# A two-layer graph network on one core: the self term of the nodes moved out of the node loop

## The chip, the cores and the metric

One NeuronCore of a Trainium2 chip runs the whole program. Its engines are TensorE (PE; matmuls, with the weight loads as PEld beside them), VectorE (DVE), ScalarE (ACT), GpSimd (POOL) and the queue engine SyncE (SP); they run on their own and meet at semaphores. The metric is the device time of one execution in microseconds (us), and lower is better. The three runs of the kernel before took 2241.53, 2242.63 and 2242.85 us; the median is 2242.63.

## The reference

Two graph layers over 100000 nodes of 64 features and 50000 edges. The edges come sorted by destination. Every layer starts with a layer norm and a maximum with zero.

```python
h = jnp.maximum(_layernorm(x, axis=-1), 0.0)
# layer 0
msg = h[src] * edge_weight[:, None]
agg = segment_sum(msg, dst, num_segments=100000)
x = x + (agg @ W_neigh + b_neigh) + h @ W_self.T      # h @ W_self.T is the self term
# layer 1: pools edge_attr by src; u[batch] is u[0] for all nodes
seg_sum, seg_max, cnt = segment_sum / segment_max / count of edge_attr over src
seg_mean = seg_sum / max(cnt, 1);  seg_max = where(cnt > 0, seg_max, 0)
z = relu(concat([seg_sum, seg_max, seg_mean, u0]) @ W1 + b1)
out = x + z @ W2 + b2
```

The second layer reads `edge_attr` and not the node features, so the output of a node is `x` + its self term + the weighted messages of its incoming edges + the pooled term of its outgoing edges.

## The kernel before, in words

Edges are taken in tiles of 128 and groups (`g`) of 8 tiles, 49 groups (`MG`). Nodes are taken in windows of 128 and groups of 8 windows, 98 groups (`WG`). The program has a first block (rank, sort and messages) and a second block (the node loop), and a third for rare overflows that has hardly any work here.

**First block.** GpSimd gathers the rows `x[src]` of the first 8 edge groups (`gather`, `EARLY = RX = 8`), then scatters all 391 tiles of edge attributes into `by_win`, ordered by window of the source node (`scatter`, L598), then gathers the other groups (L592). A scatter of group g needs its target rows, which the *rank* works out: `rank_dve`, `rank_pe` and `rank_act` run a loop over 50 groups, in which one-hot matmuls count the digits of the window numbers (histogram, h), transpose the one-hots (t), compare codes (eq, same), and a scan on VectorE and a look-up matmul turn counts into positions. After the rank, VectorE makes the first 8 message groups; once all scatters have landed it sorts the windows in 7 batches (`sort_batch`: 12 rounds of max-of-8 and the flags that drive the segment scans), and then makes the other 41 message groups as their rows come in. `message_of(g)` is: centre (L397 to L399), square on ScalarE (L417), sum (L404), root on ScalarE (L421), reciprocal times edge weight, scale and maximum (L409 to L412), four transposes on TensorE (L427), evacuation on ScalarE (L442), matmul with `W_neigh` (L806), and a split of the result into three bf16 parts (`keep`, L433 to L436), stored to `message`. A tally of destination windows (`one_hots(..., "dst")`, L797) runs in the same function and gives the table of starts at the end.

**Second block, the node loop.** A step g handles 1024 nodes. SyncE loads `x` and 8 chunks of messages; GpSimd loads the pooled edge rows, slots and flags; ring of 4. On VectorE the step is: `scans` (L997 to L1000: segment sums, maxima, means), `permute(g+1)` (L988), `norm_scale(g+1)` (L409, L412), `picks` (L1016, L1018: one-hots of destinations), `centre(g+2)`, `finish(g-1)` (L1031: adds PSUM to x), `select` (L1006: one-hots that put pooled rows in place), `value` (L1039), `norm_sum(g+2)`, `value_left` (L1045), `value_low` (L1050). On TensorE: `hidden` (L1110, the matmul with W1), `edges(g-1)` (L1141), `permute(g+1)` (L1100), `turn(g+1)` (L1151, transposes of h), `outer` (L1122, the matmul with W2), `selves(g+1)` (L1160, the self term), `neighbours` (L1131). On ScalarE: relu of the hidden layer, evacuation of the transposes, square, high part (L1209), root, middle part (L1213), and the store of the step before. Engines take their instructions in program order. What the second block reads and writes of PSUM and of the x ring is guarded by semaphores, so that an instruction in the queue holds up all behind it.

## Time and profile before

| | |
|---|---|
| profiled execution | 2241.82 us, span of its instructions 2240.1 us |
| busy, share of the span | PE 56%, PEld 48%, DVE 72%, ACT 22%, POOL 49% |
| instructions on DVE | 3568 |
| mean granted TensorE clock | 0.641 of full speed |
| HBM | read 138.46 MB, written 62.73 MB |

The busy shares are means over stages that differ. In the 40 equal slices of the page, TensorE shows nothing in slices 9 to 12 and VectorE nothing in 10 and 11, and VectorE is at eight tenths through the second half. GpSimd is at seven tenths through the first 19 slices and at two after them. How to read it: first the stages (windows of time) with the busy time of every engine in each, then inside a stage the timeline, for who starts when the other ends.

### The profile page before, as it was taken

The numbers are of one execution on the slowest core, as the hardware profiler recorded it, in microseconds if no ns is written. First come the engines' busy times: TensorE is split into PE (matmuls) and PEld (weight loads), VectorE is DVE, ScalarE is ACT, GpSimd is POOL, SyncE is SP. The second block draws the span as 40 slices with busy tenths as digits, with TensorE's granted clock in tenths as the row PEclk, the third lists the DMA queues.
The fourth block names the chain that finished last, engine by engine and source line by source line (L and its number), as shares of the span: only waits on it lengthen the run. The fifth ranks groups of instructions, "written<-read, shape, count | busy, mean of one in ns | idle before, by whom it ended". The sixth has DMA issues, their size and how long they took to land. (4 is left out here: it accounts for less than half of the span.)

```text
span 2240.1 us, 41882 instructions
## 1 busy us (share of the span) xinstructions
PE 1258.9 (56%) x14884; PEld 1073.5 (48%) x14885; DVE 1617.5 (72%) x3568; ACT 494.4 (22%) x888; POOL 1101.9 (49%) x1404
## 2 busy tenths in 40 slices
PE   4566565400001444433277777777777777777775
PEld 3444443300000333322266666667676666666665
DVE  5766767810068888766488888888888888888886
ACT  1221211100000211111132333333332333333332
POOL 7777777777773777777222222222222222232220
PEclk7565555555555555555577777777777777777776
DMA  9700000100063222222545555555555555555551
GB/s 263 95 13 13 12 13 13 55 28 13 13 154 82 76 76 79 73 61 67 104 109 122 125 119 120 125 123 121 124 119 123 123 118 124 118 123 126 119 123 32
DMA packets 405256, 203.62 MB, mean 91 GB/s; under 512 B 370375, under 2 KB 377799, under 8 KB 404407
## 3 DMA queue, kind: packets, MB, share of 16 engines
q1 hardware_dynamic: 254792, 93.02, 19.4%
q0 software_dynamic: 46976, 72.79, 14.3%
q10 hardware_dynamic: 103312, 35.54, 6.3%
q8 instruction: 101, 1.65, 0.3%
q14 instruction: 75, 0.61, 0.1%
HBM read 138.46 MB, written 62.73 MB: 90 GB/s over the span
## 5 line engine op out<-in xcount | busy, mean ns | idle before, releaser
L592 POOL DMA_INDIRECT xg_all<-in_x_dram,idx_src x391 | 385.9, 987 | 149.4 <-issue 118.3
L598 POOL DMA_INDIRECT by_win<-rows,idx_win x391 | 391.2, 1000 | 127.3 <-issue 127.3
L969 POOL DMA_DIRECT2D rows<-by_win x98 | 52.2, 532 | 782.4 <-DVE arena L1000 753.7
L1110 PE MATMUL ps<-arena,w1r 32*128 32x192 f32 x2352 | 214.2, 526 | 267.8 <-DVE arena L1000 264.6
L1110 PEld LDWEIGHTS ps<-arena,w1r 32*128 32x128 f32 x2352 | 164.6, 302 | 280.1 <-DVE arena L1000 276.6
L974 POOL DMA_DIRECT2D rows<-flag_d x392 | 214.4, 554 | 13.7 <-issue 13.6
L1122 PE MATMUL ps<-w_sb,arena 128*96 128x64 f32 x1568 | 185.8, 285 | 0.0
L1122 PEld LDWEIGHTS ps<-w_sb,arena 128*96 128x96 f32 x1568 | 184.4, 203 | 0.0
L1197 ACT ACTIVATE arena<-ps,hbias 128x768 f32<-128x768 f32 x98 | 88.3, 901 | 413.0 <-PE ps L1110 413.0
L417 ACT ACTIVATE sq<-xc 128x512 f32<-128x512 f32 x147 | 91.6, 623 | 364.7 <-DVE xc L399 364.7
L427 PE MATMUL ps<-ident,h 128*128 128x128 f32 x196 | 54.6, 434 | 174.4 <-DVE h L412 174.4
L1141 PEld LDWEIGHTS ps<-arena 96*128 96x128 bf16 x2352 | 126.4, 129 | 45.4 <-issue 45.4
L1141 PE MATMUL ps<-arena 96*128 96x64 bf16 x2352 | 140.5, 239 | 3.0 <-DVE arena L1050 3.0
L1160 PE MATMUL ps<-wsT,hT 128*128 128x128 f32 x784 | 138.9, 333 | 0.7 <-ACT hT L1202 0.7
L815 PE MATMUL ps<-ident,arena 96*112 96x96 f32 x14 | 5.0, 462 | 216.0 <-DMA arena<-by_win 216.0
L1039 DVE TENSOR_TENSOR arena<-ps,c0b 96x512 f32<-96x512 f32 x98 | 67.3, 686 | 78.6 <-PE ps L1122 71.2
L1160 PEld LDWEIGHTS ps<-wsT,hT 128*128 128x128 f32 x784 | 123.5, 239 | 1.1 <-ACT hT L1202 1.1
L714 DVE SCALAR_TENSOR_TENSOR left<-ps,iota_n 112x96 f32<-112x96 f32 x7 | 1.8, 258 | 167.7 <-PE ps L815 166.8
L1018 DVE TENSOR_TENSOR arena<-iota_n,arena 96x1024 bf16<-96x1024 f32 x98 | 119.6, 1221 | 3.4
L427 PEld LDWEIGHTS ps<-ident,h 128*128 128x128 f32 x196 | 35.0, 217 | 179.7 <-DVE h L412 179.7
L806 PE MATMUL ps<-wn,hT 128*128 128x128 f32 x392 | 101.6, 441 | 33.6 <-ACT hT L442 33.6
L1006 DVE TENSOR_TENSOR arena<-iota_n,end_n 96x1024 bf16<-96x1024 f32 x98 | 119.1, 1215 | 0.0
(191 smaller groups left out, 2840.9 us busy)
## 6 DMA issues: line engine op xcount, KB each, us to landing
rows<-message SPq DMA_DIRECT2D x784, 36.4 KB, 2.0
rows<-flag_d POOLq DMA_DIRECT2D x392, 72.0 KB, 2.6
rows<-in_x_dram SPq DMA_DIRECT2D x97, 256.0 KB, 3.1
out_dram<-rows ACTq DMA_DIRECT2D x97, 256.0 KB, 2.8
message<-m_row SPq DMA_DIRECT2D x48, 388.0 KB, 2.3
zeros<-slot_d POOLq DMA_DIRECT2D x98, 144.0 KB, 2.9
by_win<-zeros ACTq DMA_DIRECT2D x12, 808.5 KB, 10.6
arena<-by_win SPq DMA_DIRECT2D x7, 1386.0 KB, 9.4
```

What stands on the lines that cost most here:

```text
L417: nc.scalar.activation(sq[:, :, :], xc[b][:, :, :], ACT.Square).then_inc(ln["squared"], 1)
L427: last = nc.tensor.transpose(ps[bank][:, P * k:P * k + P], h[b][:, 2 * k:2 * k + 2, :].rearrange("p a c -> p (a c)"), ident[:, :])
L592: nc.gpsimd.indirect_dma_start(out=xg[g % RX][:, t % GT, :], out_offset=None, in_=x, in_offset=bass.IndirectOffsetOnAxis(ap=idx_src[:, t:t ...
L598: nc.gpsimd.indirect_dma_start(out=by_win, out_offset=bass.IndirectOffsetOnAxis(ap=idx_win[0:parts, t:t + 1], axis=0), in_=rows[0:parts, t ...
L806: last = nc.tensor.matmul(ps[1 + b][:, P * k:P * k + P], hT[b][:, k, :], wn2[:, :], start=True, stop=True)
L974: pool.dma_start(f_in[b][DE * q:DE * q + DE, :, :], two.unsqueeze(0).to_broadcast([DE, 3, 2 * SL])).then_inc(a_loaded[b], 16)
L1006: nc.vector.tensor_tensor(sel[g % 2][:, :, :], iota_n[0:SL, :].unsqueeze(1).to_broadcast([SL, GT, P]), end_n[:, g * GT:g * GT + GT].unsque ...
L1018: nc.vector.tensor_tensor(pick[c][0:CH, :, :], iota_n[0:CH, :].unsqueeze(1).to_broadcast([CH, GT, P]), near[c][:, :].unsqueeze(2).to_broad ...
L1110: last = nc.tensor.matmul(ps[z_bank[q]][:, 0:2 * SL], w1r[DE * q:DE * q + DE, j, :], part[DE * q:DE * q + DE, :], start=(j == 0), stop=(j ...
L1122: last = nc.tensor.matmul(ps[v_bank][0:SL, D * k:D * k + D], hid[:, SL * k:SL * k + SL], w2_sb[:, :], start=True, stop=True)
L1141: last = nc.tensor.matmul(ps[o_bank[c]][:, D * k:D * k + D], sel[c][:, k, :], v_part[:, k, n, :], start=False, stop=(k == GT - 1 and n == ...
L1160: nc.tensor.matmul(ps[o_bank[g % 2]][:, P * k:P * k + P], hT[g % 2][:, k, :], wsT2[:, :], start=(k == 0), stop=False)
```

## The change

The self term no longer stands in the node loop. A list of steps of two kinds is made (`steps_of`): "node" steps, 98 of them, which norm a group of 1024 nodes, multiply with `W_self` and store `x` + self term to a new table `s0_d`; and "edge" steps, the 49 message groups. Both run through the same functions (`centre`, `spread_of`, `scale_of`, `keep`; `turn` and `project` on TensorE; `square`, `relu`, `turned`, `root` on ScalarE). 61 node steps stand beside the rank, one or two per group from group 8 on; 37 stand between the edge steps behind it. A result is kept three steps after it was begun (`LAG = 3`). For node steps the scaling and the maximum are eight ScalarE instructions, one per tile of 128x64.

The rank is rewritten as well (`place_dve`, `place_pe`, `place_act`): straight code over 49 groups, the histogram is copied to four blocks of partitions, so that transposes and look-up need two wide matmuls instead of eight and sixteen narrow ones, and the tally of destinations runs in it. The sorts stand between edge steps (groups 9, 14, ... 39), the sort's row buffer is single and its other half holds node rows. The table of starts is worked out right after the rank. The node loop loads `s0_d` instead of `x` and has neither norm nor transposes nor self matmul; its `select` stands behind `value`.

The core of the diff (places with the same pattern left out):

```diff
+        s0_d = dram("s0_d", [WG * GT * P, D])
...
+            for g in range(MG):
+                chain(g)
+                same_of(g)
+                if g >= 1:
+                    place(g - 1)
+                if g + 2 < MG:
+                    spread(g + 2)
+                beside(g)
+                tallied(g)
...
+            count(0)
+            operands(0)
+            for g in range(MG):
+                if g + 1 < MG:
+                    count(g + 1)
+                second(g)
+                if g + 1 < MG:
+                    operands(g + 1)
+                beside(g)
+                if g >= 1:
+                    tally(g - 1)
...
+        def place_act(act, r, beside):
+            for g in range(MG):
+                if g >= 1:
+                    beside(g - 1)
+                b = g % 2
+                act.wait_ge(r["h"], g + 1)
...
+                for q in range(4):
+                    last = nc.scalar.activation(hist_all[b][DIGIT * q:DIGIT * q + DIGIT, :, 1:GT + 1],
+                                                h_ps.rearrange("p k l -> p l k"), ACT.Copy)
+                last.then_inc(r["w"], 1)
...
+        LAG = 3
+        NODES_AHEAD = 3
...
+            for g in range(FIRST_BESIDE, MG):
+                for _ in range(1 + g % 2):
+                    beside[g].append(todo.popleft())
...
+                def step(n):
+                    if n >= 1:
+                        scale_of(n - 1)
+                    centre(n)
+                    if n >= LAG:
+                        keep(n - LAG)
+                    spread_of(n)
...
+                for kind, g in tail_steps:
+                    step(step_of[kind, g])
+                    if kind == "edge" and g in SORT_AT:
+                        sort_batch(SORT_AT.index(g))
...
+                def relu(n):
+                    kind, g = steps[n]
+                    if kind == "edge":
+                        return
...
+                    for k in range(GT):
+                        last = nc.scalar.activation(h[b][:, k, :], xc[b][:, k, :], ACT.Relu, scale=stat[b][:, 2, k:k + 1])
+                    last.then_inc(ln["h"], 1)
...
+                def step(n):
+                    if n >= 1:
+                        relu(n - 1)
+                    square(n)
+                    if n >= 1:
+                        turned(n - 1)
+                    root(n)
...
-                        sp.dma_start(x_in[b][:, :, :], nodes_of(x, g)).then_inc(x_loaded[b], 16)
+                    sp.dma_start(x_in[b][:, :, :], nodes_of(s0_d, g)).then_inc(x_loaded[b], 16)
...
                 for g in range(WG):
                     scans(g)
                     if g + 1 < WG:
                         permute(g + 1)
-                        norm_scale(dve, own, (g + 1) % 2, cn0 + g + 2, None).then_inc(w["h"], 1)
                     picks(g)
-                    if g + 2 < WG:
-                        centre(g + 2)
                     if g >= 1:
                         finish(g - 1)
+                    value(g)
                     select(g)
-                    value(g)
-                    if g + 2 < WG:
-                        norm_sum(dve, g % 2, cn0 + g + 3)
                     value_left(g)
                     value_low(g)
...
-                        turn(g + 1)
                     outer(g)
-                    if g + 1 < WG:
-                        selves(g + 1)
                     neighbours(g)
```

How the change moves instructions, at three places. First ScalarE in the rank. Before, a group of the rank on ScalarE (`hist` and `ohT` are the copies of the histogram and of the transposed one-hots):

```order
L368 ACTIVATE hist<-ps 32x32x8
L63 ISA
L373 ACTIVATE ohT<-ps 32x512
L374 ACTIVATE ohT<-ps 32x512
L63 REGISTER_ALU
```

After, a group with two node steps and the head of the next (`h`, `sq`, `hT`, `stat`: scaled rows, squares, transposed rows, statistics of the norm):

```order
L432 ACTIVATE hist<-ps 32x32x8 x4
L438 ACTIVATE ohT<-ps 128x256
L1124 ACTIVATE h<-xc,stat 128x64 x8
L1106 ACTIVATE sq<-xc 128x512
L1132 ACTIVATE hT<-ps 128x512
L1111 ACTIVATE stat<-stat,eps_t 128x8
L1124 ACTIVATE h<-xc,stat 128x64 x8
L1106 ACTIVATE sq<-xc 128x512
L1132 ACTIVATE hT<-ps 128x512
L1111 ACTIVATE stat<-stat,eps_t 128x8
L432 ACTIVATE hist<-ps 32x32x8 x4
```

Two whole norm steps now stand between one group's histogram copies and the next one's.

Second, TensorE in the rank. Before, one group (`later` and `identh` give the comparison operands, `oh` the one-hots, `same` the comparisons, `begin_p` the table that is looked up):

```order
L326 MATMUL ps<-later,identh 128x512
L329 MATMUL ps<-identh,code_s 128x128 x4
L326 MATMUL ps<-later,identh 128x512
L329 MATMUL ps<-identh,code_s 128x128 x4
L336 MATMUL ps<-oh_lo,oh_hi 32x32 x8
L341 MATMUL ps<-identb,oh_hi 32x128 x8
L346 MATMUL ps<-ones_b,same 128x1 x8
L351 MATMUL ps<-begin_p,ohT 128x32 x16
```

After, a group with two node steps (L1042 is the self matmul, L1029 the transposes of h, L405 the tally):

```order
L379 MATMUL ps<-oh_lo,oh_hi 32x32 x8
L384 MATMUL ps<-identb,oh_hi 128x128 x2
L394 MATMUL ps<-ones_b,same 128x1 x8
L398 MATMUL ps<-begin_p,ohT 128x128 x2
L366 MATMUL ps<-later,identh 128x512
L370 MATMUL ps<-identh,code_h_win 128x128 x4
L366 MATMUL ps<-later,identh 128x512
L370 MATMUL ps<-identh,code_h_win 128x128 x4
L1042 MATMUL ps<-wsT,hT 128x128 x4
L1029 MATMUL ps<-ident,h 128x128 x4
L1042 MATMUL ps<-wsT,hT 128x128 x4
L1029 MATMUL ps<-ident,h 128x128 x4
```

The transposes of a node step stand behind the group's comparison operands and behind the self matmul of the node step before.

Third, VectorE in the node loop. Before, the part of a step between `permute` and the left part:

```order
L409 RECIPROCAL stat<-stat 128x8
L412 SCALAR_TENSOR_TENSOR h<-xc,stat 128x512
L1016 TENSOR_TENSOR arena<-rows,first_of 96x8
L1018 TENSOR_TENSOR arena<-iota_n,arena 96x1024
L397 TENSOR_REDUCE stat<-rows 128x8
L398 TENSOR_SCALAR stat<-stat 128x8
L399 TENSOR_TENSOR xc<-rows,stat 128x512
L1031 TENSOR_TENSOR rows<-rows,ps 128x512
L1006 TENSOR_TENSOR arena<-iota_n,end_n 96x1024
L1039 TENSOR_TENSOR arena<-ps,c0b 96x512
L404 TENSOR_REDUCE stat<-sq 128x8
L1045 TENSOR_TENSOR arena<-arena 96x512
```

After, the same part:

```order
L1292 TENSOR_TENSOR arena<-rows,first_of 96x8
L1294 TENSOR_TENSOR arena<-iota_n,arena 96x1024
L1304 TENSOR_TENSOR rows<-rows,ps 128x512
L1312 TENSOR_TENSOR arena<-ps,c0b 96x512
L1282 TENSOR_TENSOR arena<-iota_n,end_n 96x1024
L1318 TENSOR_TENSOR arena<-arena 96x512
```

The six instructions of the norm are gone, and the comparison against `end_n` (`select`) has moved from ahead of `value` (now L1312) to behind it.

## Rows read from the trace of the kernel before

**Rows 1.** Windows of the first half: us, busy (count) by engine, PEclk, DMA, GB/s

```profile
0.00:1083.00 1083.00, 409.82 (x3516) 310.35 (x3517) 664.82 (x1886) 147.17 (x300) 785.15 (x816) 0.53 0.27 63
480.00:560.00 80.00, 0.00 (x0) 0.00 (x0) 0.00 (x0) 0.00 (x0) 58.68 (x62) 0.50 0.06 13
```

**Rows 2.** Windows of the node loop; busy: PE, PEld, DVE, ACT, POOL

```profile
1113.74:2216.49 1102.75, 837.81 (x11228) 753.59 (x11228) 931.58 (x1644) 342.66 (x580) 303.77 (x564) 0.75 0.53 119
...
1612.77:1623.48 10.71, 7.69 (x116) 6.92 (x116) 9.64 (x19) 3.54 (x6) 3.23 (x6) 0.84 0.60 132
1623.48:1636.23 12.75, 10.61 (x116) 9.61 (x116) 9.62 (x19) 3.54 (x6) 3.23 (x6) 0.60 0.54 116
```

**Rows 3.** Timeline, a message step: start us, duration us, engine, line, operation

```profile
740.89 0.20 DVE L409 RECIPROCAL stat<-stat 128x8 f32<-128x8 f32 x1
...
741.93 0.68 DVE L397 TENSOR_REDUCE stat<-xg_all 128x8 f32<-128x512 f32 x1
742.07 1.11 PE L427 MATMUL ps<-ident,h 128*128 128x128 f32 x4 [3.48 <-DVE h L412]
...
743.22 0.60 ACT L442 ACTIVATE hT<-ps 128x512 f32<-128x512 f32 x1 [5.42 <-PE ps L427]
...
743.46 0.46 DVE L269 TENSOR_TENSOR oh_hi<-iota_d,hi_b_dst 128x256 bf16<-128x256 bf16 x1
...
743.87 2.07 PE L806 MATMUL ps<-wn,hT 128*128 128x128 f32 x8 [0.69 <-ACT hT L442]
...
745.09 0.30 ACT L421 ACTIVATE stat<-stat,eps_t 128x8 f32<-128x8 f32 x1 [0.75 <-DVE stat L404]
...
745.98 0.18 DVE L706 COPY m_row<-dst_f 128x8 f32<-128x8 f32 x1 [0.93 <-PE ps L806]
...
748.58 0.20 DVE L409 RECIPROCAL stat<-stat 128x8 f32<-128x8 f32 x1
```

**Rows 4.** Timeline of a short step of the node loop

```profile
1618.07 0.66 PE L1151 MATMUL ps<-ident,h 128*128 128x128 f32 x4
...
1618.57 1.49 PE L1122 MATMUL ps<-w_sb,arena 128*96 128x64 f32 x16
...
1620.10 0.69 DVE L1039 TENSOR_TENSOR arena<-ps,c0b 96x512 f32<-96x512 f32 x1
...
1621.48 0.69 DVE L1045 TENSOR_TENSOR arena<-arena 96x512 f32<-96x512 f32 x1
```

**Rows 5.** Timeline from the last split to the first scan, VectorE

```profile
1079.59 0.69 DVE L436 TENSOR_TENSOR m_row<-rest,m_row 128x512 bf16<-128x512 f32 x1
...
1100.81 0.67 DVE L397 TENSOR_REDUCE stat<-rows 128x8 f32<-128x512 f32 x1
...
1107.93 0.19 DVE L1054 CAST arena<-biasb 128x64 bf16<-128x64 f32 x1
...
1113.74 0.55 DVE L997 TENSOR_TENSOR_SCAN arena<-rows,ps 128x192 f32<-128x192 f32 x1
```

**Rows 6.** Timeline of one group of the rank

```profile
207.45 0.61 PE L326 MATMUL ps<-later,identh 128*128 128x512 f16 x1
...
207.56 0.42 DVE L302 TENSOR_TENSOR prod<-ps,oh_lo 128x256 f32<-128x256 f32 x1 [1.31 <-PE ps L351]
...
209.26 0.17 DVE L312 SCALAR_TENSOR_TENSOR idx_win<-pos_g,trash 128x8 f32 x1
...
209.27 0.40 PE L336 MATMUL ps<-oh_lo,oh_hi 128*32 128x32 bf16 x8
...
209.87 0.37 ACT L368 ACTIVATE hist<-ps 32x256 f32<-32x256 f32 x1 [5.22 <-PE ps L336]
210.22 1.29 DVE L287 TENSOR_TENSOR same<-ps,code_h_win 128x512 bf16<-128x512 f32 x2 [0.79 <-DVE idx_win L312]
...
211.63 0.75 DVE L293 TENSOR_TENSOR_SCAN begin<-chain_mask,hist 32x288 f32<-32x288 f32 x1
```

**Rows 7.** Window from the first sort to the end of the seventh

```profile
626.56:722.16 95.60, 9.11 (x26) 5.64 (x26) 78.22 (x351) 0.00 (x0) 52.00 (x55) 0.50 0.52 115
```

More of the change, by code:

```diff
@@ L1 @@
 import math
+from collections import deque
 from contextlib import ExitStack
@@ new lines, in beside @@
+                def beside(g):
+                    for st in beside_rank[g]:
+                        step(step_of[st])
+                place_dve(dve, own, r_win, hg, beside)
+                dve.sem_inc(made["counts"], 1)
+                dve.wait_ge(loaded["next"], 16 * 2)
+                own(nc.vector.tensor_scalar(next_i[:, :], next_i[:, :], 7, None, ALU.arith_shift_right))
+                own(nc.vector.tensor_tensor(near_f[:, :], next_i[:, :], code_i[:, 0:NT], ALU.is_lt))
+                own(nc.vector.tensor_reduce(falls[:, :], near_f[:, :], AX, ALU.add))
@@ new lines, in project @@
+                def project(n):
+                    kind, g = steps[n]
+                    bank, weights = (o_node, wsT2) if kind == "node" else (m_of[g % 2], wn2)
+                    pe.wait_ge(ln["hT"], n + 1)
+                    if kind == "node" and g >= 1:
+                        pe.wait_ge(ln["kept"], step_of["node", g - 1] + 1)
+                    if kind == "edge" and g >= 2:
+                        pe.wait_ge(ln["kept"], step_of["edge", g - 2] + 1)
+                    for k in range(4):
+                        last = nc.tensor.matmul(bank[:, P * k:P * k + P], hT[n % 2][:, k, :], weights[:, :],
@@ L860, in _, with beside @@
+                def beside(g):
+                    for st in beside_rank[g]:
+                        step(step_of[st])
+                place_act(act, r_win, beside)
+                for st in tail_steps:
+                    step(step_of[st])
+                relu(len(steps) - 1)
+                turned(len(steps) - 1)
                 act.wait_ge(made["starts"], 4)
```

600 lines of the change are left out of this document (364 added, 236 removed).

## The prediction

> **What bounds the kernel now.** I read the busy time by stages first. Up to 1083 us, in the stages that rank the edges, sort the windows and make the messages, VectorE is busy 664.8 us, so 418 us of it stand empty [rows 1]. In that half GpSimd is never out of work for long: with every other engine idle it issues 62 indirect transfers in 80 us, 1.29 us each [rows 1], and 2 x 391 of them make about 1010 us. GpSimd's queue therefore sets the end of the first half, and VectorE has room beside it, if the room can be used. From the first scan of the node loop (1113.74) to the last (2216.49) there are 97 steps in 1102.75 us, 11.37 each [rows 2]. Here no engine is full: VectorE 931.6, TensorE 837.8. The timeline of a step shows a ring: scans, hidden matmuls, second matmul, value, left part, low part, scans again. It comes in two lengths, 10.71 at a mean granted clock of 0.84 and 12.75 at 0.60 [rows 2], two short and one long in turn: (2 x 10.7 + 12.75) / 3 = 11.38. TensorE is granted 2.4 GHz or 1.2 GHz; it falls to the low level in the three us in which it waits for VectorE, and in the long step it does not come back before the second matmul.
>
> **The change in the node loop.** Gone per step are, on VectorE, two reductions and a subtract of 0.67 to 0.69, the scaling of 0.69, and two small operations, some 3 us; on TensorE the transposes (0.66 at the high clock, 1.11 at the low [rows 3, 4]) and the self matmul; on ScalarE square, root and evacuation. What is it worth on the ring? VectorE's removed work stands before `value`, where VectorE now waits for the outer matmul anyway: nothing. The self matmul comes behind the outer one and TensorE idles after it: nothing. The transposes stand between permute and outer. The outer matmul starts 1618.57, transposes 1618.07 [rows 4]; without them it can start about 0.4 earlier (0.7 in a long step, where they take 1.11). But the order is turned too: `select`, a comparison of 96x1024, stood before `value` and now stands between `value` and the left part. Before, the left part started 1.38 behind value (1620.10 to 1621.48 [rows 4]), because ScalarE's high part was waited for. With `select` between, that is 0.61 (the issue distance) + 1.14 = 1.75, 0.37 later. So the short step stays 10.7, and the long one becomes 12.75 - 0.7 + 0.37 = 12.4. The mix of short and long steps depends on how the steps fall against the clock; I keep one long in three to four: 11.2 on average, **-16 us** for 97. Bounds: all short 97 x 0.67 = -65, all long 97 x (12.4 - 11.37) = +100.
>
> Before the loop, the norms of nodes 0 and 1 (from 1100.81 to 1107.93 [rows 5]) fall away, **-7**. The last part of a message is stored at 1080.3, the first scan starts 33.5 later [rows 5]; that becomes 26.4, perhaps 3 less, since the table of starts is no longer written last.
>
> **The first half: what a node step costs beside the rank.** 98 node steps move there: 61 into groups 8 to 48 of the rank (one in the even, two in the odd, so 21 and 20), 37 between the messages. A node step is 3.1 us of VectorE: reciprocal 0.2, centring 1.53 (741.93 to 743.46 [rows 3]), the reduction of squares 0.68, the add 0.68. By busy time it would fit: 98 x 3.1 = 304 in 418. But each step is a chain over three engines with little between. VectorE reciprocal 0.2; ScalarE scales eight tiles of 128x64. No row has that form: the nearest are 128x8 at 0.30 [rows 3] and 128x512 evacuated at 0.60 [rows 3], so one takes 0.30 to 0.60, by the slope between them 0.34, and eight overlap by 0.1 each: 2.0 (bounds 1.6 and 4.8; nearest to the small one). Then transposes 1.1, evacuation 0.60, root 0.30 [rows 3], and only then the next step's reciprocal: 4.4 with handoffs.
>
> In the rank ScalarE's program has the node step *before* the histogram copies of the next group, and VectorE's next group begins by waiting for them. The ring of a group with one node step, from the end of one `place` to the next: TensorE's counts and look-up 0.7 (they wait for `place`, since the look-up's PSUM has one buffer), comparison operands 1.8 (207.45 to 209.27 [rows 6]), projection 2.07 and transposes 1.11 [rows 3] = 5.7; ScalarE evacuation 0.6, root 0.3, four histogram copies of 0.37 [rows 6] less overlap 1.3; with handoffs 8.0. Then VectorE: copy 0.2, scan 0.75, multiply 0.42, comparison 1.29, `place` 207.56 to 209.43 = 1.87 [rows 6], less overlap 4.4. Sum **12.4**. A second node step adds another chain of 4.4: **16.8**. Groups 8 to 48: 21 x 12.4 + 20 x 16.8 = 596, less 14 for stretches in which TensorE gets the high clock: 582. Groups 0 to 7 have no node step and cost VectorE's own 6.2; they start later than before, at about 30, because the weights must land first (an estimate, 20 to 40); so group 8 starts at 80 and the rank ends at **662**. GpSimd's scatters, which would be through at 97 + 391 x 1.32 = 613, wait for indices from about group 30 on and end some 10 behind the rank. GpSimd stops being the bound.
>
> **Messages, nodes and sorts.** The falls, the tallies and the starts go first: 12. Then, on VectorE, a step behind an edge step costs 1.04 scale + 1.53 + 2.60 split (745.98 to 748.58) + 0.68 + 0.34 waiting for the root (it starts as the reduction ends [rows 3]) = 6.2: before, the split stood between reduction and reciprocal and hid the root. A step behind a node step costs the chain of 4.4. 37 pairs x 10.6 + 12 x 6.2 = 467. Seven sorts, 95.6 us in a row before [rows 7], hide a root wait each: 93. Together 560, so the last message is at 1222 + 12 = 1234; its own tail (scale, transposes, evacuation, projection, split) 8: **1242**. GpSimd's gathers, 327 x 1.28 = 419 from 672, end at about 1100 and are paced by VectorE's ring of eight. The node rows (256 KB in and out a step) move on queues that are mostly empty here; nothing.
>
> Sum: first scan 1242 + 26.4 = 1268, against 1113.7: +154. With the loop's -16: +138. The span 2240.1 becomes 2378; the profiled execution has 1.7 around its span, so **2380 us**. The median of the three runs, 2242.63, stands 0.8 above the profiled 2241.82, which matters to nothing here.
>
> **Rivals.** *A, the room is used.* If the engines overlap across steps better than I read (ScalarE's copies early, relu short), VectorE's busy time is the measure: rank 49 x 6.0 + 61 x 3.1 = 483, done before the scatters end at 613; then edges 8 to 48, 31 nodes and the sorts, 41 x 5.85 + 31 x 3.1 + 93 = 429 behind the first late gather at 623: 1052, first scan 1086, 28 earlier. With the loop 2240 - 28 - 16: **2198**. For it: 418 us of empty VectorE, and the steps are written three deep. Against: every handoff above is a wait on the step just before. *B, TensorE is granted the high clock through the rank.* Its 5.7 us of a group shrink by 2.3, 41 times, and the transposes by 0.4, 37 times: 2380 - 109 = **2270**, still slower. Before, the mean in the rank was hardly above the low level. *C, the node loop loses the clock.* TensorE has nearly 2 us less work in a step of nearly the same length. In the rows a step in which the high level is missed before the outer matmul is the 12.75 one; if all were missed, 97 x 12.4 replaces 97 x 11.2: **2496**. The decision falls where the hidden matmuls and the edges behind them no longer win the high level. The Trainium skill, TensorE: Matmul & The Clock Gate, "What's actually happening", says that the low clock is the default and activity releases it; by that, taking the transposes and self matmuls out speaks for C. The trace agrees so far that the fall comes after idling; whether the matmuls left suffice no row shows. *D, the change does nothing on balance*: A's first half lost in part, within 0.2%.
>
> **How the numbers follow.** Forecast 0.55, its own range 2300 to 2440 (relu at 1.6 or 2.6 us: 98 times, -40 or +60; the loop's mix -49 to +60 around). A 0.24, B 0.10, C 0.08, D 0.03. About 0.2% is what a measurement here can tell from no change. Faster 0.24, same 0.03, slower 0.73. The range must reach into A: 2190 leaves some 0.11 of it outside, 2450 leaves C: 0.19 in all.
>
> **What would show it.** In the profile after: histogram copies on ScalarE that start right behind a root, in groups some 12 and 17 us apart; GpSimd idle during the scatters waiting for VectorE's index, with the last scatter near 670; first scan near 1268; eight scalings of 128x64 in about 2.0; loop steps of 10.7 and 12.4, with VectorE waiting for the outer matmul longer than before. The forecast is wrong if the groups with two node steps take 11 us or less, or if the scatters still end near 613; it is wrong in the loop if the short step is under 10.3 or no two lengths are left.

## The result, and the profile of the changed kernel

The changed kernel takes 2423.31 us (median of 4 runs, 2419.35 to 2424.96), the kernel before 2242.74 (4 runs beside it, 2241.53 to 2244.96). The ratio is 1.0801, 95% interval 1.0783 to 1.082: slower by 181 us where 137 were forecast. The page of the profiled execution begins so:

```profile
span 2420.6 us, 39452 instructions
...
PE 1291.7 (53%) x13560; PEld 1085.0 (45%) x13561; DVE 1604.2 (66%) x3454; ACT 697.3 (29%) x1766; POOL 1095.5 (45%) x1407
```

VectorE, the busiest engine, does 1604 us of work in a span of 2421. That is 13 us less than before (1617.5), and no engine is full. The loss therefore is not VectorE's work but waiting, and the stages say where. The windows (us, busy and count of PE, PEld, DVE, ACT and POOL, PEclk, DMA share, GB/s) of the first half up to the first scan of the node loop, of the rank, of the stretch of messages, nodes and sorts, and of the loop:

```profile
0.00:1308.16 1308.16, 599.33 (x3384) 477.36 (x3385) 936.46 (x2371) 485.53 (x1472) 792.61 (x843) 0.56 0.41 94
...
80.00:726.00 646.00, 304.23 (x2054) 240.78 (x2055) 411.72 (x1035) 272.11 (x865) 386.31 (x392) 0.55 0.28 61
...
740.00:1285.00 545.00, 265.15 (x1061) 215.30 (x1061) 459.61 (x1152) 193.23 (x554) 322.02 (x328) 0.53 0.43 110
...
1308.16:2396.90 1088.74, 685.70 (x10064) 601.62 (x10064) 657.20 (x1067) 209.56 (x291) 302.94 (x564) 0.71 0.53 121
```

The first scan comes at 1308.16 instead of 1113.74 [rows 1, 5]: 194 us later. The loop takes 1088.74 for its 97 steps instead of 1102.75 [rows 2]: 14 us less, 11.22 a step, with 274 us less work on VectorE. In the rank, GpSimd is busy for 386 of 646 us, and its group of scatters now names VectorE's index as what it waits for (busy, mean ns | idle before, most of it for):

```profile
L792 POOL DMA_INDIRECT by_win<-rows,idx_win x391 | 386.6, 989 | 259.7 <-DVE idx_win L340 137.4
...
L1124 ACT ACTIVATE h<-xc,stat 128x64 f32<-128x64 f32 x784 | 197.8, 334 | 221.2 <-DVE stat L896 221.2
```

The distances between the starts of `place` are 5.7 to 5.9 for groups without a node step, 12.7 for one with one, and 18.1 to 20.4, mostly 19, for one with two (the first ones after group 7 are shorter, 10.1 and 15.3). The timeline of a group with two, which runs from 478.90 to 498.03, from its second reciprocal (L896) on (start, duration, engine, line, operation, [idle before, released by]):

```profile
487.46 0.20 DVE L896 RECIPROCAL stat<-stat 128x8 f32<-128x8 f32 x1 [2.69 <-ACT stat L1111]
487.70 2.02 ACT L1124 ACTIVATE h<-xc,stat 128x64 f32<-128x64 f32 x8 [0.27 <-DVE stat L896]
...
489.34 0.68 DVE L910 TENSOR_TENSOR arena<-arena,ps 128x512 f32<-128x512 f32 x1
...
490.17 2.00 PE L1042 MATMUL ps<-wsT,hT 128*128 128x128 f32 x8 [3.56 <-DVE arena L910]
...
491.96 1.06 PE L1029 MATMUL ps<-ident,h 128*128 128x128 f32 x4
...
493.06 0.60 ACT L1132 ACTIVATE hT<-ps 128x512 f32<-128x512 f32 x1 [2.82 <-PE ps L1029]
493.55 0.29 ACT L1111 ACTIVATE stat<-stat,eps_t 128x8 f32<-128x8 f32 x1
493.74 1.51 ACT L432 ACTIVATE hist<-ps 32x256 f32<-32x256 f32 x4
...
495.29 0.20 DVE L320 COPY hist<-begin 128x32 f32<-128x32 f32 x1 [3.66 <-ACT hist L432]
...
498.03 0.41 DVE L334 TENSOR_TENSOR prod<-ps,oh_lo 128x256 f32<-128x256 f32 x1
```

Two things are to be seen. The scalings (L1124) are done at 489.72, but the transposes of the node (L1029) start at 491.96: on TensorE the self matmul (L1042) of an earlier node stands in front of them, and it waits for VectorE's `keep` (L910, ends 490.02), which frees the one PSUM buffer of the result. And VectorE waits 3.66 us for the histogram copies (L432), which on ScalarE stand behind evacuation and root of the last node step. VectorE is busy for 6.45 of these 10.57 us:

```profile
487.46:498.03 10.57, 3.67 (x24) 3.15 (x24) 6.45 (x14) 5.08 (x16) 2.65 (x3) 0.79 0.26 56
```

A short step of the loop, to be laid beside [rows 4]:

```profile
1617.17 1.57 PE L1387 MATMUL ps<-w_sb,arena 128*96 128x64 f32 x16
...
1618.78 0.69 DVE L1312 TENSOR_TENSOR arena<-ps,c0b 96x512 f32<-96x512 f32 x1 [1.28 <-PE ps L1387]
1619.38 1.21 DVE L1282 TENSOR_TENSOR arena<-iota_n,end_n 96x1024 bf16<-96x1024 f32 x1
...
1620.52 0.68 DVE L1318 TENSOR_TENSOR arena<-arena 96x512 f32<-96x512 f32 x1
```

From value to left part it is 1.74 us with `select` between, 1.38 before. Steps are 10.6, 11.0 or 12.3 long.

### The profile page after: what moved, and what is told of

Same layout as the page of the kernel before. It is cut to its first block and busy times, and to the rows that moved or that the text cites. A ratio compares the mean times of both kernels' runs of the same rounds, so it can differ in the third digit from the quotient of the medians.

```text
span 2420.6 us, 39452 instructions
## 1 busy us (share of the span) xinstructions
PE 1291.7 (53%) x13560; PEld 1085.0 (45%) x13561; DVE 1604.2 (66%) x3454; ACT 697.3 (29%) x1766; POOL 1095.5 (45%) x1407
## 3 DMA queue, kind: packets, MB, share of 16 engines
q0 software_dynamic: 46976, 72.79, 12.7%
## 5 line engine op out<-in xcount | busy, mean ns | idle before, releaser
L1375 PE MATMUL ps<-arena,w1r 32*128 32x192 f32 x2352 | 223.5, 544 | 409.1 <-DVE arena L1276 409.1
L1375 PEld LDWEIGHTS ps<-arena,w1r 32*128 32x128 f32 x2352 | 173.8, 318 | 422.4 <-DVE arena L1276 415.8
L1042 PE MATMUL ps<-wsT,hT 128*128 128x128 f32 x784 | 199.7, 436 | 120.5 <-DVE arena L910 100.2
L1124 ACT ACTIVATE h<-xc,stat 128x64 f32<-128x64 f32 x784 | 197.8, 334 | 221.2 <-DVE stat L896 221.2
L1042 PEld LDWEIGHTS ps<-wsT,hT 128*128 128x128 f32 x784 | 173.7, 326 | 149.1 <-issue 116.7
L1029 PE MATMUL ps<-ident,h 128*128 128x128 f32 x588 | 158.8, 426 | 98.9 <-ACT h L1124 80.6
L1304 DVE TENSOR_TENSOR rows<-rows,ps 128x512 f32<-128x512 f32 x98 | 67.4, 688 | 183.7 <-PE ps L1408 183.7
L1312 DVE TENSOR_TENSOR arena<-ps,c0b 96x512 f32<-96x512 f32 x98 | 67.3, 687 | 181.1 <-PE ps L1387 181.1
L1029 PEld LDWEIGHTS ps<-ident,h 128*128 128x128 f32 x588 | 117.7, 224 | 116.2 <-ACT h L1124 91.6
L1448 ACT ACTIVATE arena<-arena 96x512 bf16<-96x512 f32 x98 | 61.7, 630 | 359.7 <-DVE arena L1312 359.7
L1132 ACT ACTIVATE hT<-ps 128x512 f32<-128x512 f32 x147 | 86.9, 591 | 187.4 <-PE ps L1029 187.4
L1042 PE MATMUL ps<-wn,hT 128*128 128x128 f32 x392 | 94.9, 418 | 64.9 <-ACT hT L1132 64.9
```

What stands on the lines that cost most here:

```text
L1029: last = nc.tensor.transpose(hT_of[kind][:, P * k:P * k + P], h[n % 2][:, 2 * k:2 * k + 2, :].rearrange("p a c -> p (a c)"), ident[:, :])
L1042: last = nc.tensor.matmul(bank[:, P * k:P * k + P], hT[n % 2][:, k, :], weights[:, :], start=True, stop=True)
L1124: last = nc.scalar.activation(h[b][:, k, :], xc[b][:, k, :], ACT.Relu, scale=stat[b][:, 2, k:k + 1])
L1132: nc.scalar.activation(hT[n % 2][:, :, :], hT_of[kind][:, :].rearrange("p (k c) -> p k c", c=P), ACT.Copy).then_inc(ln["hT"], 1)
L1375: last = nc.tensor.matmul(ps[z_bank[q]][:, 0:2 * SL], w1r[DE * q:DE * q + DE, j, :], part[DE * q:DE * q + DE, :], start=(j == 0), stop=(j ...
```

## The experiments

Each is the changed kernel with one edit, unless it says otherwise. Ratios are to the kernel before, run beside it.

**Transposes first.** In TensorE's part of a node step:

```diff
-                    if n >= 2:
-                        project(n - 2)
                     if n >= 1:
                         turn(n - 1)
+                    if n >= 2:
+                        project(n - 2)
```

> The changed kernel, with one edit: in a node step TensorE does the transposes of the node before first and the self matmul of the node before that behind them. Theory (the groups of the rank with two node steps miss the forecast because the second step's transposes stand on TensorE behind a self matmul that waits for VectorE's `keep`): that wait and the 2.0 us of the matmul leave the ring; even groups 12.7 -> about 10.7, odd ones 19.0 -> about 15, the rank ends some 100 to 120 us earlier (place(48) near 610 to 625), the whole near 2310. Rival (the second step is simply a longer chain: relu, transposes and root cost more than I put them at, the self matmul lies beside them): groups stay at 12.7 and 19.0, total 2415 to 2425.

Measured: 2332.39 us (2331.96 to 2334.07), ratio 1.0397 [1.038, 1.0414]. Groups with one node step 10.9 to 11.0, with two 16.4, last `place` at 637.9 instead of 725.6. Both lengths fell, so the self matmul and its wait were on the ring, as the theory had it; those with two came to 16.4, not 15. The timeline shows what is late next in such a group:

```profile
401.76 2.02 ACT L1124 ACTIVATE h<-xc,stat 128x64 f32<-128x64 f32 x8 [4.92 <-DVE stat L896]
...
403.84 1.12 PE L1029 MATMUL ps<-ident,h 128*128 128x128 f32 x4 [0.45 <-ACT h L1124]
...
404.00 0.37 SPq L682 DMA_DIRECT2D s_d<-arena  x1
...
404.40 0.58 SPq L676 DMA_DIRECT2D arena<-in_x_dram  x1
...
405.81 0.20 DVE L896 RECIPROCAL stat<-stat 128x8 f32<-128x8 f32 x1 [0.79 <-ACT stat L1111]
...
407.94 0.69 DVE L882 TENSOR_REDUCE stat<-arena 128x8 f32<-128x512 f32 x1 [1.93 <-DMA arena<-in_x_dram]
...
412.73 0.32 DVE L320 COPY hist<-begin 128x32 f32<-128x32 f32 x1 [1.11 <-ACT hist L432]
```

The transposes now follow the scalings by 0.1, and 1.93 us go to a new wait: the next node's rows are not there yet. Their load (L676, issued at 404.40) stands in SyncE's program behind the store of an earlier result (L682), which can be issued only after `keep`, and the rows are there 3.5 us later, so a faster group runs into it. One thing more changed with the order: the mean granted clock from 80 us to the last `place` is 0.62 here, against 0.55 in the changed kernel (0.59 with the histogram copies first, 0.61 up to 580 us with all three edits). In the group shown, 16.4 long, the first transposes still took 1.12 us, as at the low level; how much of the 91 us is the faster clock is not separated.

**Histogram copies first.** In ScalarE's loop over the groups:

```diff
             for g in range(MG):
-                if g >= 1:
-                    beside(g - 1)
                 b = g % 2
...
                 nc.scalar.activation(ohT4[b], t4_ps, ACT.Copy).then_inc(r["ohT"], 1)
+                if g >= 1:
+                    beside(g - 1)
```

> The changed kernel, with one edit: ScalarE's program makes the histogram copies of group g before the node steps of group g - 1, not behind them. Theory: the copies leave the ring and VectorE's scan of the next group no longer waits for the root; but ScalarE's scalings of the node then start up to 1.5 us later. VectorE's own in-order program still waits for the node's centring, so the group shortens by what the copies cost, 1.5 to 3 us in each of 41 groups: -60 to -120 us, total 2300 to 2360. Rival (the ring is closed through VectorE's node steps and TensorE's self matmul, not through the copies; they only change places): less than 0.5 us a group, total within 20 us of 2423.

Measured: 2285.48 us (2282.88 to 2286.76), ratio 1.0186 [1.0169, 1.0203]: 138 less, beyond the expected range. Groups 9.1 and 15.5 instead of 12.7 and 19, 3.5 to 3.6 each, last `place` at 587.1, last scatter at 611. More goes than the 1.5 us of the copies; by the order of ScalarE's program the next group no longer waits for evacuation and root of the last node step either, some 0.9 us, and what the rest is was not taken apart. The timeline of this kernel still has the self matmul's wait, in an even group now without harm:

```profile
312.79 0.68 DVE L910 TENSOR_TENSOR arena<-arena,ps 128x512 f32<-128x512 f32 x1
313.62 2.04 PE L1042 MATMUL ps<-wsT,hT 128*128 128x128 f32 x8 [0.74 <-DVE arena L910]
315.10 0.19 DVE L320 COPY hist<-begin 128x32 f32<-128x32 f32 x1
315.45 1.06 PE L1029 MATMUL ps<-ident,h 128*128 128x128 f32 x4
```

VectorE's next group (L320) starts before the transposes do.

**Select first.** In VectorE's node loop:

```diff
-                    value(g)
                     select(g)
+                    value(g)
                     value_left(g)
```

> The changed kernel, with one edit: in the node loop `select` stands before `value` on VectorE again, as it did before the change. Theory (select between value and the left part costs 0.37 us on the ring): first scan unchanged at 1308, short step 10.6 -> about 10.3, mean 11.2 -> 10.85, total 2385 to 2395. Rival 1 (VectorE waits for the outer matmul anyway and the left part waits for ScalarE's high part as late as before): unchanged, 2420 to 2425. Rival 2 (a shorter step leaves TensorE less or more time at the high clock, so the mix of short and long steps moves): anything from all steps short (10.3, total 2333) to all long (12.0, 2500).

Measured: 2326.18, 2328.4, 2470.07 and 2481.3 us; no ratio is given for so two-fold a result. In the profiled run (2328.4) every step from the second on is 10.2 to 10.4 long:

```profile
1308.89:2303.23 994.34, 610.22 (x10064) 536.49 (x10064) 665.46 (x1067) 209.48 (x291) 302.97 (x564) 0.83 0.58 133
```

That is 94 us less than with `select` behind value, of which the theory's 0.37 a step explains 36. The rest is that no step is long any more: the mean granted clock of the loop is 0.83, against 0.71. The other two runs are some 150 us longer, at a mean clock of 0.54 and 0.55 over the whole run against 0.68; they have no trace, and that the loop holds the difference (1.5 a step) is inferred. Rival 2 holds: the mix of step lengths moved, both ways, and by more than what was taken off the ring. That the clock is the cause, and not only goes with it, is argued.

**All three.**

> The changed kernel with three edits of order: transposes before self matmul on TensorE, histogram copies before the node steps on ScalarE, and in the node loop `select` before `value` as before the change. If the three act on different waits, gains add: rank -150 to -220 us, node loop -0.37 a step = -36: total 2170 to 2240, near or below the kernel before. Rival (once the first wait is gone the next ring, relu and transposes and root between two node steps, sets the group at 12 to 13 with two steps and 8 to 9 with one): rank ends near 530 to 560, then GpSimd's scatters, 613, are the measure, and the total is about 2270 to 2300.

Measured: 2182.25 us (2181.45 to 2182.4), ratio 0.9727 [0.9711, 0.9743]: faster than the kernel before. The total lies in the expected range, but not by the expected parts: the rank gave less than 150 and the loop far more than 36, so that is partly luck. The gains in the rank don't add. Last `place` at 580.4 (-145, where -88 and -139 were had apart), groups 9.2 and 15.2, last scatter at 609, where GpSimd ends by its own pace. Up to the first scan the gain is 147, and the other 93 are the loop:

```profile
0.00:580.00 580.00, 310.48 (x2275) 240.74 (x2277) 457.25 (x1168) 295.17 (x908) 436.43 (x470) 0.65 0.47 99
1161.18:2157.04 995.86, 612.33 (x10064) 538.56 (x10064) 665.37 (x1067) 209.48 (x291) 302.98 (x564) 0.83 0.58 133
```

**No node step beside the rank.**

```diff
-        FIRST_BESIDE = EARLY
+        FIRST_BESIDE = MG
```

> The changed kernel with no node step beside the rank: all 98 stand between the messages. The rank then runs at the 5.75 us a group of the changed kernel's groups 0 to 7 (place(48) near 325), and the GpSimd scatters end near 613 again. Theory (a node step costs 5.2 us as one of a pair between the messages, whether a second one follows or not, since its chain of three engines is not overlapped): 98 x 5.2 + 49 x 5.6 + 93 + 12 = 890 behind 325, less what waits for the gathers (edge 8 cannot start before the scatters end at 613, when 30 of 98 steps may be done): last message 1215 to 1300, total near 2360 to 2440. Rival (beside the messages VectorE is simply busy, 5.85 + 3.1 a pair): 98 x 3.1 + 49 x 5.85 + 93 = 684, end at about 1075 to 1130, total 2200 to 2270.

Measured: 2536.43 us (2534.7 to 2537.04), ratio 1.1311 [1.1292, 1.133]. The rank is as expected (5.7 a group, last `place` at 322.5), scatters end at 606. A miss in the tail: two node steps and an edge step take 16.7 us, not 16, and where the gathers stop the tail for 180 us before edge 8, only about 15 node steps have been dealt out, not 30. The order of the tail is fixed, so VectorE can't use the wait. Moving node steps beside the rank saved 113 us against this.

**No node steps.** The node steps and the loads of their rows are left out of both places, and the loop loads x as it is, so that the self term is missing from the result:

```diff
-            todo = deque(("node", j) for j in range(WG))
+            todo = deque()
...
-                    sp.dma_start(x_in[b][:, :, :], nodes_of(s0_d, g)).then_inc(x_loaded[b], 16)
+                    sp.dma_start(x_in[b][:, :, :], nodes_of(x, g)).then_inc(x_loaded[b], 16)
```

> The changed kernel with the node steps left out: the self term is not computed at all and the node loop loads x as it is, so this is the cost of everything but the moved work. Theory (the first half's loss is all node steps): scatters end at 613, gathers at about 1032, last message near 1045, first scan near 1070, 240 less than the changed kernel's 1308; loop as there, 11.2 a step; total 2175 to 2185. Rival (part of the loss is in the other edits of the first half, the two message steps of lag, the tables of starts written first): first scan at 1090 or later, total over 2200.

Measured: 2167.3 us (2166.22 to 2168.45), ratio 0.9665 [0.9649, 0.9681]. First scan at 1052.26, 256 before that of the changed kernel; loop 1090.4 us, to within 2 us the same. Both are earlier than expected, the first scan by 18 us and the total by some 8. The whole loss of the first half, and more, is the node steps; the other edits of the half, with the norms ahead of the loop gone, gained 61 us on the kernel before.

```profile
0.00:1052.26 1052.26, 305.60 (x2208) 226.99 (x2209) 649.65 (x1784) 162.59 (x394) 781.22 (x843) 0.57 0.29 67
```

Against the changed kernel VectorE has 287 us less work here [936.46 above], TensorE 294, ScalarE 323, and the stretch is 256 shorter: nearly a whole VectorE's worth, as if nothing had been hidden.

**The loop alone.** The kernel before, with norm and self term left out of its node loop and `select` where it stood (edit of VectorE's part, without the norms ahead of the loop; the other engines' are like it):

```diff
-                        norm_scale(dve, own, (g + 1) % 2, cn0 + g + 2, None).then_inc(w["h"], 1)
...
-                        centre(g + 2)
...
-                        norm_sum(dve, g % 2, cn0 + g + 3)
```

> The kernel before with norm and self term left out of the node loop (the self term is not computed, x is added as loaded), `select` kept in front of `value`: what the removal in the loop is worth by itself. First half unchanged. Theory (VectorE's and ScalarE's removed work is worth nothing, the transposes 0.4): short step 10.7 -> 10.2 to 10.3. By the first changed-order run the loop then settles in one of two patterns, all steps 10.2 (total 1107 + 97 x 10.2 + 24 = 2125) or all long, 11.8 (2275), or the mix of before (11.0: 2200); which of them, I cannot tell from rows. Rival (the removed VectorE work was on the ring): short step under 9.5, total under 2060.

Measured: 2126.26, 2125.5, 2125.65 and 2279.33 us; ratio of the first three 0.948 [0.9461, 0.9499]. Both of the theory's first two totals came up, to within 5 us. The short step falls from 10.71 to 10.24, 0.47: the transposes' 0.4 and hardly more, for 266 us of VectorE work less in the loop (665.42 against 931.58 [rows 2]). But that is not all that the loop gave back: its 97 steps take 996.33 us instead of 1102.75, 106 less. The shorter short step makes 46 of it; the other 60 is that the long steps are gone, in the runs that stay in the short pattern.

```profile
1104.91:2101.24 996.33, 612.81 (x10064) 538.69 (x10064) 665.42 (x1066) 209.43 (x291) 302.97 (x564) 0.82 0.58 132
```

**Matmuls that nobody reads.** To keep TensorE at work before the hidden matmuls:

```diff
+                def keep_busy():
+                    for _ in range(10):
+                        nc.tensor.matmul(ps[z_bank[0]][0:D, 256:256 + D], w2_sb[:, :], w2_sb[:, :], start=True, stop=True)
...
                     outer(g)
                     neighbours(g)
+                    keep_busy()
```

> The changed kernel with ten extra matmuls of 64x64 in each step of the node loop, in the 3.9 us in which TensorE waits for the scans; nobody reads their result. Theory (steps come in lengths of 10.6, 11.0 and 12.3 only because TensorE drops to 1.2 GHz while it idles and comes back late): all steps 10.6, granted clock of the loop near 1.0, loop 97 x 10.6 = 1028, total near 2365. Rival 1 (long steps come from something else, transfers or the edge matmuls' wait): mix unchanged, 2420. Rival 2 (the extra matmuls at the low clock delay the hidden matmuls): steps over 12.3, total over 2500.

Measured: 2466.8 us (2457.86 to 2469.9), ratio 1.0996 [1.0968, 1.1024]: slower. My theory fell. The mean step went from 11.22 to 11.67, the mean granted clock from 0.71 to 0.61, although TensorE was busy for 950 us instead of 686 (199 of the 264 more are the extra matmuls themselves; the outer ones grew from 189 to 254 us in all, since more of them ran at the low level). Windows from this run, first the whole loop:

```profile
1305.52:2437.96 1132.44, 949.95 (x12004) 852.44 (x12004) 656.99 (x1067) 209.62 (x291) 302.99 (x564) 0.61 0.52 117
...
1606.50:1610.50 4.00, 2.10 (x32) 1.97 (x34) 3.30 (x8) 0.63 (x1) 0.00 (x0) 0.88 0.46 93
1610.90:1630.50 19.60, 18.15 (x221) 16.18 (x214) 10.06 (x15) 3.69 (x5) 6.07 (x12) 0.50 0.56 124
1630.80:1634.50 3.70, 1.83 (x31) 1.69 (x34) 2.97 (x8) 0.63 (x1) 0.13 (x1) 0.93 0.45 93
```

TensorE is busy for 18.15 of 19.6 us and is granted 1.2 GHz throughout; the high level (2.4 GHz) comes in the two stretches in which it is half idle. In the changed kernel itself there is a stretch of 8.5 us in which it never pauses, at the low level:

```profile
1623.80:1632.30 8.50, 8.50 (x104) 7.55 (x104) 3.68 (x6) 1.40 (x2) 3.22 (x6) 0.50 0.51 118
```

Rival 2, too late hidden matmuls, is not it either: they start at once behind the scans, as ever; the outer matmuls are the ones that miss the high level (2.82, 2.83 and 2.82 us in the three steps from 1599 us on).

**The same with select first.**

> The changed kernel with `select` in front of `value`, and the ten matmuls of 64x64 that nobody reads in TensorE's empty stretch before the hidden matmuls. The same filling in the changed order made more steps long, not fewer (11.6 mean against 11.2). Theory (what a step costs depends on where the outer and the hidden matmuls fall against the high stretches, and the filling takes a high stretch that these would have had): the pattern of equal 10.24 steps goes, mean 11.2 to 11.8, total 2420 to 2475, in every run alike. Rival (the filling was harmful only in the order with `select` behind `value`; here it secures the high clock): all steps 10.2, total 2325 in every run and no run near 2475.

Beside this kernel and the next one the kernel before took 2619 us, not 2242 (later 2629), on the same chip on which it had taken 2244 beside the first four experiments. The traces of the kernels run beside it show that what stands ahead of the node loop was slower; of the kernel before there is no trace from that time. So totals are read only against it. Measured: 2562.55 us (2560.51 to 2567.27), ratio 0.9799 [0.9763, 0.9835], and the loop is not longer than in the kernel without the extra matmuls:

```profile
1542.17:2536.33 994.16, 737.96 (x12004) 657.69 (x12004) 665.42 (x1066) 209.55 (x291) 303.21 (x564) 0.83 0.58 133
```

The four totals lie within 7 us, and in the profiled run the steps are 10.2: the theory fell, and the rival holds for the loop (its total of 2325 can't be compared). The very matmuls that lengthened the loop with `select` behind value do no harm here.

**One node step in each group.** The three edits of order, and another deal of the node steps:

```diff
-                for _ in range(1 + g % 2):
-                    beside[g].append(todo.popleft())
+                beside[g].append(todo.popleft())
...
-                while todo and (MG - 1 - g) * left < len(todo) * (MG - 1):
+                while todo and (g < EARLY and len(todo) > left - 2 * (g + 1) or g >= EARLY and
+                                (MG - 1 - g) * (left - 2 * EARLY) < len(todo) * (MG - 1 - EARLY)):
...
-        FIRST_BESIDE = EARLY
+        FIRST_BESIDE = 0
```

> The three edits of order together (transposes first, histogram copies first, select first), and the node steps dealt out otherwise: one in each of the 49 groups of the rank, none twice; in the tail two to each of the first 8 edge steps, whose rows were gathered early, the other 33 to edge steps 8 to 48. Theory (one node step beside a group of the rank costs 3.4, a second 6, one between messages 5): place(48) near 49 + 48 x 9.1 = 486, scatters end 613 as without nodes, since GpSimd sets them; then 41 edge steps with 33 nodes 10.5 each, 8 at 6.2, sorts 93: last split near 1115, first scan near 1135, loop all at 10.24: total 2150 to 2165. Rival (VectorE stalls between its early edge steps and the end of the scatters, or the groups with a node cost more while weights and zeros are still arriving): 2175 to 2195, no better than with the deal as changed.

Measured, beside the same kernel before: 2486.06, 2494.05 and 2494.85, and 2612.5 to 2638.49 for the other three; ratio of the three 0.9519 [0.9474, 0.9564]. Many groups are 9.1 to 9.3 long, as expected, but in between are groups of 10 to 28, most often one in two of 16.7, and the last `place` comes at 746.5 instead of 486. In the long ones VectorE and TensorE stand still without a partner that is at work (TensorE's rows are two of eight such matmuls, which elsewhere go four in 0.63 us):

```profile
233.42 0.69 DVE L884 TENSOR_TENSOR xc<-arena,stat 128x512 f32<-128x512 f32 x1
243.67 0.69 DVE L910 TENSOR_TENSOR arena<-arena,ps 128x512 f32<-128x512 f32 x1 [9.56 <-remote]
```

```profile
240.17 0.26 PE L370 MATMUL ps<-identh,code_h_win 128*128 128x128 f16 x1 [1.53 <-issue]
242.25 0.26 PE L370 MATMUL ps<-identh,code_h_win 128*128 128x128 f16 x1 [1.82 <-issue]
```

The expectation therefore is neither borne out nor refuted: it was for an undisturbed rank. Nor is it shown that the disturbance alone makes the long groups. The kernel with `select` first and the extra matmuls, run at the same time, has its usual 12.7 and 19 from group 10 on; this one has long groups to the end of the rank, here and in the two later traces of kernels with this deal.

**Once more, and with the extra matmuls.**

> The same kernel as the one with one node step in every group of the rank, on a chip on which the kernel before takes its usual 2242 (in the first run of it the kernel before took 2619 too, and the first half of both was slowed). Theory as there: place(48) near 486, scatters end near 613, first scan near 1135, loop steps 10.24: 2150 to 2165. Of the runs some may have a loop of 11.8 a step, some 150 us more, as three of six had there. Rival: the groups cost more than 9.1 or VectorE stalls before the scatters end: 2175 to 2195.

> The same, and in the node loop the ten matmuls of 64x64 that nobody reads. Theory (with `select` in front of `value` the filling takes away the second pattern of the loop, as four equal runs of the kernel with both showed): all runs within 5 us of each other, loop steps 10.22, total as the kernel beside it in its short pattern, 2150 to 2165. Rival (the four equal runs were luck: one in 16 if each had an even chance): one or more runs some 150 us longer.

The kernel before took 2628.7 us, on another chip, so again neither total can be held against the expectation. Without the extra matmuls: four runs at 2489.41 to 2512.41, three at 2655.54 to 2660.72; ratio of the four 0.9498 [0.9465, 0.9531]. With them: six runs at 2488.76 to 2513.18, none some 150 us longer, ratio 0.9505 [0.947, 0.9539]; they are 24 us apart and not the expected 5, and the mean step of the profiled run is 10.26. The profiled run of the first is one of the long ones, so the two patterns of one and the same kernel can be laid side by side; the loop of this run, that of the short pattern from the time before (on the other chip), and that with the extra matmuls:

```profile
1497.26:2634.52 1137.26, 798.26 (x10064) 705.28 (x10064) 665.57 (x1067) 209.56 (x291) 303.30 (x564) 0.54 0.52 116
```

```profile
1472.53:2469.09 996.56, 612.97 (x10064) 538.62 (x10064) 665.50 (x1067) 209.50 (x291) 303.22 (x564) 0.82 0.58 133
```

```profile
1489.07:2484.58 995.51, 742.62 (x12004) 661.85 (x12004) 665.52 (x1067) 209.50 (x291) 303.33 (x564) 0.82 0.59 133
```

In the first two VectorE's, ScalarE's and GpSimd's work are the same; TensorE's differs by its clock, 0.54 against 0.82, and the loop by 141 us. Whether the new deal of the node steps is worth anything where nothing is disturbed stays open: 2182 is the best total that was measured against an undisturbed 2242.

## Why the prediction was right, and by how much it was short

**What set the end of each half: right.** The rank rings through node steps and histogram copies, GpSimd stops being the bound, the messages follow at the pace of VectorE's chain, and the loop gives back little. The parts, measured against the working:

- Groups without a node step 5.7 to 5.9 (6.2), but they begin 10 us later than I put it: `place` of group 7 at 89.6, where I had 80.
- Groups with one node step 12.7 (12.4); the first (10.1) and the last (5.7) are shorter, so that all 21 together are 3 us under the sum.
- **Groups with two 19.1 (16.8): the step that failed.** I made the second node step "another chain of 4.4"; it took 19.1 - 12.7 = 6.4. Its transposes stand behind the self matmul of an earlier node, and that waits for `keep`: 2.2 us between the end of the scalings and the transposes in the timeline above, and 42 us over the sum in the 20 groups. The experiment that turns the two round takes that gap away, brings such a group to 16.4 and the whole down by 91 (at a granted clock that rose as well). I had charged the projection once, in the first step's ring ("projection 2.07 and transposes 1.11"), and forgot it in the second.
- "Less 14 for stretches in which TensorE gets the high clock": nothing came of that; the mean granted clock of the rank is 0.55. Rival B had no more ground than this.
- Last `place` at 725.6 (662): 42 + 14 + 10 - 3 = 63.
- From there to the end of the last split 564 us, where 580 was worked out (pairs 10.5 against 10.6): -16. From there to the first scan 18.5 (26.4): -8. (The last gather ended at 1214, not at about 1100; the sum didn't use it.)
- Loop 11.22 a step (11.2), short 10.6 and long 12.3 (10.7 and 12.4), with a middle one of 11.0 that I had not foreseen: -14 (-16). That the two agree so well is luck: the mix of long and short steps was assumed to stay, and the experiments show that one instruction's place moves it, and 93 us with it.

Sum: 2378 + 63 - 16 - 8 + 2 = 2419; the span is 2420.6. The misses in the messages and before the loop took back 24 of the 63 that were missed in the rank.

**The unknown price.** The scaling of 128x64 on ScalarE takes 334 ns, eight of them 2.02 us; the slope between two rows gave 0.34 and 2.0.

**The rivals.** *A, the room is used*, did not come. With the histogram copies first the scatters end at 611, as A has it, but even with all three edits the last `place` comes at 580 (A: 483) and the first scan at 1161 (A: 1086). That the total is then 2182, 16 below A's 2198, is the loop's doing (996 us) and not A's. The evidence that I held against A ("every handoff is a wait on the step just before") was right, though part of those waits belongs to this order of the programs only. *C, the loop loses the clock*, did not come in the changed kernel, but it is no idle threat: the kernels with `select` first have runs that are some 150 us longer, and the one of them that has a trace shows steps of 11.7 on average at a granted clock of 0.54.

**Where the loop's gain went.** The removed VectorE work was worth next to nothing on the short step, as argued (266 us of it gone, 0.47 gained, in the kernel with the bare loop). Of that 0.47 the turned order of `select` took 0.37 back by the rows (1.74 against 1.38), which leaves the 0.1 between 10.7 and 10.6. What I had not seen is that with `select` in its old place the same removal also ends the long steps in most runs: the loop gives back 106 us there and 14 here. Of the 92 between them 36 are the 0.37 of `select`, 97 times; the rest is the mix of step lengths.

## What to carry to other kernels

Work that would fit into an engine's idle time by its busy sum can cost nearly its full length when each piece is a chain over three in-order engines (here 256 us for 287 us of VectorE work, beside a half in which VectorE had been idle for 418): the place of each piece in every engine's program must be checked for what stands in front of it and what that waits for. Put the short operation that frees another engine (a transposition, a copy of a histogram) ahead of the long one whose buffer is still being read; two such swaps, and one in the loop, turned 8% slower into 2.7% faster. When a second unit of moved work is added to a stage, work its ring out anew with all its operations, instead of adding the part of the chain that was missing for the first.

## What the runs showed of the hardware

- TensorE's granted clock did not follow its work. Granted 1.2 GHz for 19.6 us with 18.15 us busy, and 2.4 GHz in stretches half idle; 264 us more busy time in the loop lowered the mean from 0.71 to 0.61. The Trainium skill, TensorE: Matmul & The Clock Gate, "What's actually happening", says that the low clock is the default and that activity releases it; these rows, by the busy time that the profile counts, don't agree with that as a rule for when the high clock comes. What does decide it here no run shows.
- A loop can keep step with the clock. In the traces of three kernels with different programs ahead of it (the kernel before with a bare loop, select first, all three edits) the last 80 steps are 10.240 us each, to 0.005; with select first the stretches of the high clock begin 10.24 apart too (1611.48, 1621.72, 1631.96). Which of the two sets the other is not shown. The same kernels, started again, sometimes take some 150 us more: 1 of 4, 2 of 4 and 0 of 4 runs, and with one node step in each group 3 of 6 and 3 of 7. The one long run with a trace has steps of 11.7 on average at a granted clock of 0.54. With the ten extra matmuls and `select` first no run was long, of 4 and of 6. By that they seem to hold the short pattern, but ten runs are few, and a reason is not shown.
- At two times, on two chips, the kernel before took 376 and 386 us more, and the kernels beside it had slower stages ahead of the node loop (select first with the extra matmuls by 233 up to its first scan), with engines idle on no visible partner (9.56 us before one addition, 1.5 to 1.8 between single matmuls), while their short loops stayed at 10.2 to 10.3 a step. The cause stays open.
